# Dilated attention and channel attention on one core: who adds the nine neighbour products

## The chip, the core and the metric

The kernel runs on one core of a Trainium2 chip. Five engines work side by side, each with its own list of instructions, and wait for one another by semaphores: TensorE (PE, matmuls; PEld is its weight load), VectorE (DVE), ScalarE (ACT), GpSimd (POOL) and SyncE (SP, which issues transfers). The metric is the device time of one execution in microseconds (us).

## The reference

`x` is 8 images of 128 channels and 16 by 16 positions. Two residual layers follow each other:

```
x = x + _L0_conv_ref(_gn(x), w_qkv, w_gate, b_gate)
x = x + _L1_conv_ref(_gn(x), W_qkv, b_qkv, W_proj, b_proj)
```

`_gn` is a group norm over groups of 4 channels. The first layer projects to q, k and v (128 channels each), cut into four branches of 32 channels with dilations 1, 2, 4 and 8. In a branch every position looks at a 3 by 3 neighbourhood at that dilation:

```
attn = softmax(einsum('bhdn,bhdkn->bhnk', q, unfold3x3(k)) * scale)
out  = einsum('bhnk,bhdkn->bnhd', attn, unfold3x3(v))
```

The second `einsum` is the place of the change: for each position nine products of a probability and a shifted v are added up. The branch's output is multiplied by a gate (a softmax over the branches of pooled x). The second layer is an attention over channels (heads of 32 channels, 32 by 32 scores), with a projection before and after.

## The kernel before, in words

The 8 images are worked in two halves (`ph` 0 and 1) of four images (`j` 0 to 3). In the first layer a tile's 128 partitions are four images times the 32 channels of one branch `s`, and its free dimension is the 256 positions. One branch of one half is called a **unit** here, written (ph,s).

For a unit, TensorE writes the softmax probabilities, spread over the channels, into PSUM in three chunks (`spread`, L842), one per column shift. VectorE multiplies each chunk with shifted v (`multiply_pv`, L596) and leaves the nine products in the SBUF tile `pv[s]`. Both halves use the same four `pv` tiles. Then eight additions per unit (`additions`, L71) sum the nine products into `acc`: on GpSimd (L333 to L340) or on VectorE (`add_neighbours`, L616). `POOL_SUMS` = (4, 2) says that GpSimd does all four units of half 0 and the first two of half 1; VectorE does (1,2) and (1,3). Outside the middle the shifted windows are smaller where the dilation is larger: the additions cover 240 to 256 elements in branch 0, 224 to 256 in branch 1, 144 or 192 in branch 2 and 64 or 128 in branch 3.

`restore` (L863) brings `acc` back to the layout of the residual, one image per PSUM bank and 128 channels: for each image four matmuls, one per branch, with a 128 by 32 piece of the identity as the weights. Four such matmuls lie side by side in column groups. `first_residual` (L627, two images: one group `g`) adds the image and the result and takes the channel sum. ScalarE takes the sum of squares (`squares`), TensorE averages over the norm's groups (`group_stats`), VectorE computes the variance (`second_variance`, L508 to L516), GpSimd the power -1/2 (`rsqrt`, L302), VectorE the norm's bias (`second_norm_bias`), and ScalarE or VectorE the normed image. From there the second layer runs per group: `project_second`, `transpose`, `attention`, shift, exp and divide, `fuse`, `finish`, `second_residual`, and the store of one image.

Groups 0 and 1 come from half 0 and are worked while half 1 of the first layer still runs; groups 2 and 3 come from half 1, and their chain is the end of the program.

The order on each engine is written out by hand: the lists at L669 to L758 for VectorE and L923 to L1024 for TensorE. On GpSimd it is the loop over halves and units, with `RSQRT_AFTER` naming the addition behind which the `rsqrt` of groups 0 and 1 is put; GpSimd takes its instructions in order, so an addition behind an `rsqrt` waits until that has run. `keep_clock` (L765) are matmuls whose result nobody reads, written where TensorE would otherwise stand idle.

## Time and profile before

| what | value |
|---|---|
| time, median of 3 runs | 84.69 us (84.1 to 85.41) |
| the profiled execution | 84.39 us, its span 82.6 us |
| busy: PE, DVE, ACT, POOL | 67.3, 69.6, 30.7, 42.4 us |
| granted TensorE clock | 1.00 in every slice |
| GpSimd's additions | from 30.84 to 61.88 us |
| first and last addition of VectorE | 59.24 and 65.12 us |
| first matmul of the second `restore` | 65.51 us |

Times in the trace are counted from the start of the span; 1.8 us of the execution's own time lie outside the span. A row gives start and length; rows that follow one another on an engine overlap by some hundredths, since a length holds the pipeline's fill too, so that costs are better taken from start to start. The trace records two matmul rows for each fp32 matmul of the program. "idle before <-releaser" says how long the engine stood and for what.

### The profile page before, as it was taken

To read this page: it belongs to the slowest core of one execution; us is meant where nothing else is said; L and a number is where in the kernel's file an instruction comes from. 1 tells how busy PE (TensorE), PEld (TensorE's weight loads), DVE (VectorE), ACT (ScalarE), POOL (GpSimd) and SP (SyncE) were. 2 spreads that over 40 slices of the span, in tenths; PEclk is the share of its full clock that TensorE was granted. 3 is DMA by queue.
4 is the path that set the end of the run, shared out by engine and by line. 5 is a ranking of instruction groups with operands and counts; after the bars stand their busy time and mean duration, and the time that the engine had idled before them with its cause. 6 is when DMAs were issued, how large, how long until landed. Compare 5 with 4: busy or idle time off the path is not lost.

```text
span 82.6 us, 2228 instructions
## 1 busy us (share of the span) xinstructions
PE 67.3 (81%) x888; PEld 49.0 (59%) x888; DVE 69.6 (84%) x191; ACT 30.7 (37%) x97; POOL 42.4 (51%) x82
## 2 busy tenths in 40 slices
PE   0099899799867979999966797979999787999960
PEld 0099695476433656686855664667685545677830
DVE  1087679999999999999999698889999999857980
ACT  4396599615537000000030004220993155485320
POOL 7104279108700009999999999899990003300000
PEclk9999999999999999999999999999999999999999
DMA  0995004000000000000000000000000000011244
GB/s 5 315 356 150 1 0 100 5 0 0 8 0 0 4 12 0 0 0 0 12 0 0 0 0 0 0 8 0 0 0 0 0 8 4 0 63 64 71 158 159
DMA packets 3019, 3.11 MB, mean 38 GB/s; under 512 B 320, under 2 KB 2752, under 8 KB 3008
## 3 DMA queue, kind: packets, MB, share of 16 engines
q1 hardware_dynamic: 2576, 2.69, 9.9%
q10 hardware_dynamic: 432, 0.26, 1.4%
q8 instruction: 7, 0.11, 0.6%
q14 instruction: 4, 0.03, 0.1%
HBM read 1.91 MB, written 1.05 MB: 36 GB/s over the span
## 4 chain that ended last, share of the span: by engine, by line
DVE 42%; POOL 29%; PE 13%; issue 5%; DMA 4%; ACT 2%; POOLq 1%; ACTq 0%
DVE qk L572 17%; POOL acc L340 13%; POOL pv L340 12%; PE ps L763 11%; DVE pv L613 5%; DMA xt<-x_dram 4%; POOL rstd L305 4%; DVE acc L625 4%; DVE pv L625 3%; DVE x L632 2%; PE ps L898 2%; DVE ssum L589 1%; ACT pT L402 1%; DVE x L658 1%; POOLq L99 1%
## 5 line engine op out<-in xcount | busy, mean ns | idle before, releaser
L763 PE MATMUL ps<-prob,sel 64*128 64x192 f32 (+6 forms) x192 | 17.7, 313 | 2.9 <-DVE pv L613 1.9
L613 DVE TENSOR_TENSOR pv<-ps,v 128x128 f32<-128x128 f32 (+7 forms) x32 | 17.1, 569 | 1.7 <-PE ps L763 0.9
L763 PE MATMUL ps<-xn,wp 128*32 128x256 f32 (+1 forms) x208 | 16.4, 382 | 1.7 <-DVE shifted L582 1.2
L763 PEld LDWEIGHTS ps<-prob,sel 64*128 64x128 f32 x192 | 13.7, 186 | 6.9 <-DVE pv L613 4.8
L340 POOL TENSOR_TENSOR pv<-pv 128x240 f32<-128x240 f32 (+3 forms) x24 | 14.6, 617 | 0.1
L572 DVE TENSOR_TENSOR qk<-q,k 128x720 f32<-128x720 f32 (+7 forms) x24 | 13.9, 646 | 0.1
L763 PE MATMUL ps<-xt 128*128 128x128 f32 x56 | 10.6, 334 | 4.1 <-DMA xt<-x_dram 4.1
L763 PEld LDWEIGHTS ps<-xn,wp 128*32 128x32 f32 (+1 forms) x208 | 9.7, 116 | 6.3 <-DVE shifted L582 1.7
L340 POOL TENSOR_TENSOR acc<-acc,pv 128x256 f32<-128x256 f32 (+4 forms) x20 | 12.6, 635 | 0.5
L305 POOL TENSOR_TENSOR rstd<-gvar,mhalf 128x2 f32<-128x2 f32 (+1 forms) x6 | 4.9, 824 | 14.9 <-DVE gvar L516 14.9
L763 PEld LDWEIGHTS ps<-xt 128*128 128x128 f32 x56 | 8.6, 230 | 5.2 <-DMA xt<-x_dram 4.1
L763 PE MATMUL ps<-qk,cs 128*32 128x192 f32 (+6 forms) x176 | 7.8, 302 | 0.9 <-ACT v L385 0.5
L340 POOL TENSOR_TENSOR acc<-pv 128x256 f32<-128x256 f32 x4 | 2.9, 728 | 8.5 <-DVE pv L613 8.5
L395 ACT ACTIVATE expd<-shifted 128x576 f32<-128x576 f32 x2 | 1.4, 684 | 15.8 <-DVE shifted L582 15.8
L402 ACT ACTIVATE pT<-x 128x256 f32<-128x256 f32 x8 | 3.3, 411 | 10.4 <-DVE x L632 10.4
L763 PEld LDWEIGHTS ps<-qk,cs 128*32 128x32 f32 x176 | 4.7, 109 | 3.6 <-ACT v L385 1.0
L541 DVE TENSOR_REDUCE sums<-xt 128x1 f32<-128x256 f32 x8 | 2.8, 413 | 2.8 <-DMA xt<-x_dram 2.8
L763 PE MATMUL ps<-p,mT 128*128 128x256 f32 x16 | 4.6, 399 | 0.3 <-ACT mT L429 0.2
L763 PE MATMUL ps<-acc,cs 128*32 128x256 f32 x64 | 4.1, 383 | 0.7 <-issue 0.6
L360 ACT ACTIVATE xn<-xt 128x256 f32<-128x256 f32 x8 | 3.2, 404 | 2.0 <-DMA xt<-x_dram 2.0
L415 ACT ACTIVATE p<-ps,wp 128x256 f32<-128x256 f32 x8 | 3.4, 473 | 1.1 <-PE ps L763 1.1
L572 DVE TENSOR_TENSOR qk<-ps,k 128x128 f32<-128x128 f32 (+4 forms) x12 | 3.8, 379 | 0.0
(75 smaller groups left out, 94.0 us busy)
## 6 DMA issues: line engine op xcount, KB each, us to landing
xt<-x_dram SPq DMA_DIRECT2D x4, 256.0 KB, 3.6
out_dram<-x SPq DMA_DIRECT2D x8, 128.0 KB, 1.8
wp<-wpack_dram SPq DMA_DIRECT2D x1, 325.0 KB, 5.6
sel<-selc_dram SPq DMA_DIRECT2D x4, 64.0 KB, 3.9
cs<-consts_dram ACTq DMA_DIRECT2D x1, 130.0 KB, 3.3
cs<-consts_dram ACTq DMA_DIRECT2D x2, 64.0 KB, 2.6
```

Source lines behind the costliest of these rows:

```text
L305: nc.gpsimd.tensor_tensor(rstd[:, bs], gvar[:, bs], mhalf[:, bs], ALU.pow).then_inc(rstd_ready, 1)
L340: nc.gpsimd.tensor_tensor(o, a, b, ALU.add).then_inc(added, 1)
L360: nc.scalar.activation(xn1[:, b // GB, b % GB, :], xt[:, b, :], ACT.Square, accum_out=sums[:, b, 1:2]).then_inc(square_ready, 1)
L402: nc.scalar.activation(pT[:, g, 2 * i:2 * i + 2, :].rearrange("p t n -> p (t n)"), x1[:, b, :], ACT.Square, accum_out=sums1[:, b, 1:2]).th ...
L415: nc.scalar.activation(p1[:, g, i, :], ps[:, BANK[g] + i, 0:N], ACT.Identity, bias=wp[:, W_B1:W_B1 + 1]).then_inc(p1_copied, 1)
L541: nc.vector.tensor_reduce(sums[:, b, 0:1], xt[:, b, :], AX.X, ALU.add).then_inc(sum_ready, 1)
L572: last = nc.vector.tensor_tensor(o, a, b, ALU.mult)
L613: last = nc.vector.tensor_tensor(o, a, b, ALU.mult)
L625: nc.vector.tensor_tensor(o, a, b, ALU.add).then_inc(dve_added, 1)
L632: nc.vector.scalar_tensor_tensor(out=x1[:, b, :], in0=ps[:, BANK[g] + i, 0:N], scalar=1.0, in1=xt[:, b, :], op0=ALU.mult, op1=ALU.add, acc ...
L763: return nc.tensor.matmul(o, w, m, start=start, stop=stop)
L898: last = nc.tensor.transpose(ps[:, BANK[g] + i, P * t:P * t + P], p1[:, g, i, P * t:P * t + P], ident)
```

## The change

Unit (0,3) is no longer added on GpSimd. TensorE adds it: the nine products are matmul operands with the identity as weights, accumulated in PSUM (`sum_units`, `neighbours`). Unit (1,2) goes from VectorE to GpSimd, so that GpSimd does (0,0), (0,1), (0,2), (1,0), (1,1), (1,2), and VectorE only (1,3). `restore` is gone: `sum_units` writes all branches of a half, with 32 by 32 pieces of the identity (32 partitions in, 32 out) instead of 128 by 32. The second `rsqrt` on GpSimd moves in front of unit (1,1). Both residuals of half 0 move forward on VectorE, and 9 of the `keep_clock` matmuls of the later part go: 3 of 6 in front of `spread(1, 0, 0)`, 3 around `spread(1, 2, 2)`, 3 in front of the second sum.

```diff
-POOL_SUMS = (ND, 2)
+POOL_SUMS = (3, 3)
+TENSOR_SUMS = ((3,), ())
-RSQRT_AFTER = ((1, 0, 4), (1, 1, 0))
+RSQRT_AFTER = ((1, 0, 4), (1, 0, 7))
...
+        def neighbours(s):
+            return [(3 * ci + ri, *valid_rows(s, ri), *columns(DIL[s], ci)[:2])
+                    for ci in CENTRE_FIRST for ri in CENTRE_FIRST]
...
-            def restore(g):
...
-                for i in range(GB):
-                    for s in range(ND):
-                        last = mm(ps[32 * s:32 * s + 32, BANK[g] + i, 0:N],
-                                  ident[:, 32 * (first + i):32 * (first + i) + 32], acc[:, ph, s, :])
-                    last.then_inc(restored, 1)
+            def sum_units(ph, units):
+                if ph == 0:
+                    pe.wait_ge(shift_ready, PHASES)
+                    pe.wait_ge(qk_ready, ND * PHASES)
+                else:
+                    pe.wait_ge(pv_ready, 12 * PHASES)
+                parts = []
+                for s in units:
+                    if s in TENSOR_SUMS[ph]:
+                        pe.wait_ge(pv_ready, 12 * ph + 3 * s + 3)
+                        parts.append([(pv[s], slot * N, r0, r1, c0, c1) for slot, r0, r1, c0, c1 in neighbours(s)])
+                        continue
+                    if s < POOL_SUMS[ph]:
+                        pe.wait_ge(added, ADDS * (sum(POOL_SUMS[:ph]) + s + 1))
+                    else:
+                        pe.wait_ge(dve_added, ADDS * (added_before(ph, s) + 1))
+                    parts.append([(acc, (ph * ND + s) * N, 0, H, 0, W)])
+                for n in range(max(len(part) for part in parts)):
+                    for s, part in zip(units, parts):
...
+                        for j in range(SLOTS):
+                            rows = slice(32 * j, 32 * j + 32)
+                            last = mm(view(ps, 512 * (BANK[2 * ph] + j) + r0 * W + c0, dims, 32 * s, 32),
+                                      ident[rows, rows], view(t, offset + r0 * W + c0, dims, 32 * j, 32),
+                                      start=(n == 0), stop=(n == len(part) - 1))
+                            if s == (2, 3)[ph]:
+                                last.then_inc(restored, 1)
...
-            pe.wait_ge(pv_ready, 12 * PHASES)
-            keep_clock(3, BANK[2])
-            restore(2)
-            restore(3)
+            sum_units(1, (0, 1, 2, 3))
```

The instructions move at three places. Each listing gives the line, the operation, output and input, the shape, and the semaphores waited for.

**GpSimd, half 1.** L340 and L350 are the additions, L305 and L315 the `rsqrt` of a group of images. Before, from the first addition of (1,0) on:

```order
L340 TENSOR_TENSOR pv0<-pv0 128x16x15 [waits pv_ready]
L305 TENSOR_TENSOR rstd<-gvar,mhalf 128x2 [waits var_ready]
L340 TENSOR_TENSOR acc<-acc,pv0 128x16x15 [waits added]
L340 TENSOR_TENSOR pv0<-pv0 128x16x15 [waits added]
L340 TENSOR_TENSOR acc<-acc,pv0 128x16x15 [waits added]
L340 TENSOR_TENSOR acc<-pv1 128x256 [waits pv_ready]
L305 TENSOR_TENSOR rstd<-gvar,mhalf 128x2 [waits var_ready]
L340 TENSOR_TENSOR pv1<-pv1 128x16x14 [waits pv_ready]
```

And now:

```order
L350 TENSOR_TENSOR pv0<-pv0 128x16x15 [waits pv_ready]
L315 TENSOR_TENSOR rstd<-gvar,mhalf 128x2 [waits var_ready]
L350 TENSOR_TENSOR acc<-acc,pv0 128x16x15 [waits added]
L350 TENSOR_TENSOR pv0<-pv0 128x16x15 [waits added]
L350 TENSOR_TENSOR acc<-acc,pv0 128x16x15 [waits added]
L315 TENSOR_TENSOR rstd<-gvar,mhalf 128x2 [waits var_ready]
L350 TENSOR_TENSOR acc<-pv1 128x256 [waits pv_ready]
L350 TENSOR_TENSOR pv1<-pv1 128x16x14 [waits pv_ready]
```

The first `rsqrt` keeps its place behind the fifth addition of (1,0), and the second comes one addition earlier; behind unit (1,1) the eight additions on `pv2` follow now.

**VectorE, from the third chunk of (1,0) to the first variance.** L613 and L625 are products, L632 and L644 residuals, L513 to L516 and L523 to L526 the variance. Before:

```order
L613 TENSOR_TENSOR pv0<-ps,v0 128x48x15 [waits spread_ready] x2
L613 TENSOR_TENSOR pv1<-ps,v1 128x768 [waits added,spread_ready,proj_copied]
L632 SCALAR_TENSOR_TENSOR x1,sums1<-ps,xt 128x256 [waits restored] x2
L613 TENSOR_TENSOR pv1<-ps,v1 128x48x14 [waits spread_ready]
L513 TENSOR_TENSOR gst<-ps,signs 128x2x2 [waits gstats_ready]
L515 TENSOR_TENSOR gsq<-gst 128x2 [waits dve_settled]
L516 SCALAR_TENSOR_TENSOR gvar<-gst,gsq 128x2 [waits dve_settled]
```

And now:

```order
L625 TENSOR_TENSOR pv0<-ps,v0 128x48x15 [waits spread_ready] x2
L644 SCALAR_TENSOR_TENSOR x1,sums1<-ps,xt 128x256 [waits restored] x2
L625 TENSOR_TENSOR pv1<-ps,v1 128x768 [waits added,spread_ready,proj_copied]
L644 SCALAR_TENSOR_TENSOR x1,sums1<-ps,xt 128x256 [waits restored] x2
L625 TENSOR_TENSOR pv1<-ps,v1 128x48x14 [waits spread_ready]
L523 TENSOR_TENSOR gst<-ps,signs 128x2x2 [waits gstats_ready]
L525 TENSOR_TENSOR gsq<-gst 128x2 [waits dve_settled]
L526 SCALAR_TENSOR_TENSOR gvar<-gst,gsq 128x2 [waits dve_settled]
```

The residual of group 1 stood behind the first variance and stands in front of it now.

**TensorE, around the third chunk of (1,0).** Before, from `spread(1, 0, 2)` on, which followed `spread(1, 0, 1)` directly:

```order
L763 MATMUL ps<-prob,sel 128x3x4x15 [waits pv_ready]
L763 MATMUL ps<-prob,sel 128x3x4x15 x3
L763 MATMUL ps<-prob,sel 128x3x4x16 [waits pv_ready]
L763 MATMUL ps<-prob,sel 128x3x4x16 x3
L763 MATMUL ps<-acc,cs 32x256 [waits qk_ready,shift_ready,added]
L763 MATMUL ps<-acc,cs 32x256 x7
```

And now:

```order
L774 MATMUL ps<-prob,sel 128x3x4x15 x3
L774 MATMUL ps<-pv3,cs 32x256 [waits pv_ready,qk_ready,shift_ready]
L774 MATMUL ps<-pv3,cs 32x256 x3
L774 MATMUL ps<-pv3,cs 32x128 x8
L774 MATMUL ps<-pv3,cs 32x16x8 x4
L774 MATMUL ps<-pv3,cs 32x8x8 x8
L774 MATMUL ps<-pv3,cs 32x16x8 x4
L774 MATMUL ps<-pv3,cs 32x8x8 x8
L774 MATMUL ps<-prob,sel 128x3x4x15 [waits pv_ready]
L774 MATMUL ps<-prob,sel 128x3x4x15 x3
L774 MATMUL ps<-acc,cs 32x256 [waits added,qk_ready,shift_ready]
L774 MATMUL ps<-acc,cs 32x256 x11
```

The 36 matmuls that add unit (0,3) stand between the second and the third chunk of (1,0), and 12 matmuls for the units (0,0) to (0,2) stand behind the third.

## Rows read from the trace of the kernel before

**Rows 1.** The page: busy time, the span in slices.
```profile
PE 67.3 (81%) x888; PEld 49.0 (59%) x888; DVE 69.6 (84%) x191; ACT 30.7 (37%) x97; POOL 42.4 (51%) x82
...
PEclk9999999999999999999999999999999999999999
```

**Rows 2.** The chain of waits in order of time: start, length, what.
```profile
48.80 0.47 POOL acc L340
...
49.31 0.96 DVE pv L613
...
52.90 0.71 POOL rstd L305
...
63.14 0.79 DVE pv L613 x4
...
65.12 0.29 DVE acc L625
...
66.21 0.86 DVE x L632 x4
...
79.45 0.92 DVE x L658 x2
```

**Rows 3.** Timeline of GpSimd: start, length, engine, line, instruction, tiles.
```profile
36.42 0.73 POOL L340 TENSOR_TENSOR acc<-pv 128x256 f32<-128x256 f32 x1
...
42.27 0.49 POOL L340 TENSOR_TENSOR pv<-pv 128x144 f32<-128x144 f32 x1
...
44.73 0.99 POOL L340 TENSOR_TENSOR pv<-pv 128x144 f32<-128x144 f32 x1
...
45.80 1.00 POOL L340 TENSOR_TENSOR acc<-acc,pv 128x192 f32<-128x192 f32 x2
...
55.68 0.73 POOL L340 TENSOR_TENSOR acc<-pv 128x256 f32<-128x256 f32 x1
...
58.36 1.31 POOL L340 TENSOR_TENSOR pv<-pv 128x224 f32<-128x224 f32 x2
...
59.63 0.80 POOL L340 TENSOR_TENSOR acc<-acc,pv 128x224 f32<-128x224 f32 x1
...
61.20 0.68 POOL L340 TENSOR_TENSOR acc<-acc,pv 128x224 f32<-128x224 f32 x1
```

**Rows 4.** Timeline of VectorE, the second half's products, sums and additions.
```profile
46.46 1.77 DVE L613 TENSOR_TENSOR pv<-ps,v 128x768 f32<-128x768 f32 x2 [0.68 <-issue]
...
48.40 1.87 DVE L613 TENSOR_TENSOR pv<-ps,v 128x720 f32<-128x720 f32 x2 [0.17 <-PE ps L763]
...
50.18 0.41 DVE L632 SCALAR_TENSOR_TENSOR x<-ps,xt 128x256 f32<-128x256 f32 x1
...
51.20 0.86 DVE L613 TENSOR_TENSOR pv<-ps,v 128x672 f32<-128x672 f32 x1 [0.25 <-PE ps L763]
...
52.09 0.16 DVE L513 TENSOR_TENSOR gst<-ps,signs 128x4 f32<-128x4 f32 x1
...
59.82 0.78 DVE L625 TENSOR_TENSOR pv<-pv 128x144 f32<-128x144 f32 x1
...
65.12 0.29 DVE L625 TENSOR_TENSOR acc<-acc,pv 128x128 f32<-128x128 f32 x1
```

**Rows 5.** Timeline of TensorE, matmul rows; x counts two rows a matmul.
```profile
4.05 2.07 PE L763 MATMUL ps<-xt 128*128 128x128 f32 x8 [4.05 <-DMA xt<-x_dram]
...
43.05 1.60 PE L763 MATMUL ps<-xt 128*128 128x128 f32 x12
...
45.43 1.53 PE L763 MATMUL ps<-prob,sel 64*128 64x192 f32 x16 [0.78 <-DVE prob L592]
...
49.31 1.07 PE L763 MATMUL ps<-acc,cs 128*32 128x256 f32 x16
...
63.68 0.33 PE L763 MATMUL ps<-pT 128*32 128x32 f32 x16 [0.20 <-ACT pT L420]
...
65.51 1.93 PE L763 MATMUL ps<-acc,cs 128*32 128x256 f32 x32 [0.58 <-issue]
```

More of the change, by code:

```diff
@@ L244, in of_phase, with added_before @@
             return slice(ph, B, PHASES)
+        def neighbours(s):
+            return [(3 * ci + ri, *valid_rows(s, ri), *columns(DIL[s], ci)[:2])
+                    for ci in CENTRE_FIRST for ri in CENTRE_FIRST]
+        def added_before(ph, s):
+            return len([u for u in range(POOL_SUMS[ph], s) if u not in TENSOR_SUMS[ph]])
         def operands(ph, s, n, target, slot):
@@ L602, in multiply_pv @@
                 dve.wait_ge(spread_ready, c + 1)
-                if ph and chunk == 0:
+                if ph and chunk == 0 and s in TENSOR_SUMS[0]:
+                    dve.wait_ge(restored, SLOTS)
+                elif ph and chunk == 0:
                     dve.wait_ge(added, ADDS * (s + 1))
@@ L608, in multiply_pv @@
                     o = view(pv[s], (3 * ci + ri) * N + r0 * W + c0, [[dri * N + dr * W, n], [W, rows], [1, nc_]])
-                    if ci == 1 and n == 1:
+                    if ci == 1 and n == 1 and s not in TENSOR_SUMS[ph]:
                         o = view(acc, (ph * ND + s) * N, [[W, rows], [1, nc_]])
@@ L616, in add_neighbours @@
             def add_neighbours(ph, s):
-                done = ADDS * (s - POOL_SUMS[ph])
+                done = ADDS * added_before(ph, s)
                 for n, (target, slot, after) in enumerate(additions(s)):
@@ L715, in _ @@
                 multiply_pv(1, 0, i)
+            first_residual(0)
             multiply_pv(1, 1, 0)
-            first_residual(0)
+            first_residual(1)
             multiply_pv(1, 1, 1)
             second_variance(0)
-            first_residual(1)
             multiply_pv(1, 1, 2)
@@ L728, in _ @@
             multiply_pv(1, 3, 0)
-            add_neighbours(1, 2)
             for i in range(1, 3):
@@ L861, in spread @@
                 last.then_inc(spread_ready, 1)
-            def restore(g):
-                ph, first = g // 2, GB * (g % 2)
-                if g % 2 == 0:
-                    pe.wait_ge(added, ADDS * sum(POOL_SUMS[:ph + 1]))
-                    if POOL_SUMS[ph] < ND:
-                        pe.wait_ge(dve_added, ADDS * (ND - POOL_SUMS[ph]))
+            def sum_units(ph, units):
                 if ph == 0:
-                    pe.wait_ge(shift_ready, g + 1)
+                    pe.wait_ge(shift_ready, PHASES)
@@ new lines, in sum_units @@
+                for n in range(max(len(part) for part in parts)):
+                    for s, part in zip(units, parts):
+                        if n >= len(part):
+                            continue
+                        t, offset, r0, r1, c0, c1 = part[n]
+                        dims = [[W, r1 - r0], [1, c1 - c0]]
+                        for j in range(SLOTS):
[5 more added lines that the diff above has]
+                                last.then_inc(restored, 1)
@@ L964, in _ @@
             spread(0, 3, 2)
-            keep_clock(6)
-            for i in range(3):
+            keep_clock(3)
+            for i in range(2):
                 spread(1, 0, i)
-            spread(1, 1, 0)
-            restore(0)
-            spread(1, 1, 1)
+            sum_units(0, (3,))
+            spread(1, 0, 2)
+            sum_units(0, (0, 1, 2))
+            for i in range(2):
+                spread(1, 1, i)
             group_stats(0)
-            restore(1)
             spread(1, 1, 2)
@@ L976, in _ @@
                 spread(1, 2, i)
-            keep_clock(2, BANK[1] + 1)
-            spread(1, 2, 2)
-            keep_clock(1, BANK[1] + 1)
-            spread(1, 3, 0)
             for i in range(2):
                 project_second(0, i)
+            spread(1, 2, 2)
             for i in range(2):
                 project_second(1, i)
-            for i in range(2):
-                transpose(0, i)
-            for i in range(1, 3):
-                spread(1, 3, i)
+            spread(1, 3, 0)
+            transpose(0, 0)
+            spread(1, 3, 1)
+            transpose(0, 1)
+            spread(1, 3, 2)
             transpose(1, 0)
```

1 line of the change is left out of this document (removed).

## The prediction

> **What bounds the kernel now.** I read the page's busy times first: no engine is full, VectorE and TensorE come nearest, and GpSimd works half of the span [rows 1]. So the order of waits counts, and I went on to the chain of waits. From 31.66 on it lies on GpSimd's additions, without a break but for some hundredths, down to the last one of half 0, which ends at 49.27 (48.80 + 0.47). After a detour over the first residuals and their norm it takes GpSimd again from 52.90, and from 57.8 on VectorE with its own additions up to 65.41 (65.12 + 0.29); then follow the residuals of group 2 at 66.21 and the tail, which ends with the last residual, 79.45 + 0.92 [rows 2]. What releases the tail is the first matmul of the second `restore`, at 65.51 [rows 5]: it needs all additions of half 1, on both engines. GpSimd's were done at 61.88 (61.20 + 0.68) [rows 3], so VectorE was late by 3.5 us. The question is when the later of the two is done after the change.
>
> **GpSimd's first saving.** Up to the end of unit (0,2) nothing changes. In the row of two additions at 45.80, which ends at 46.80, the second is the first of unit (0,3) [rows 3]; of the 1.00 I give it 0.41 and the longer one the rest. So (0,2) ends at 46.4, and (0,3) took from there to 49.27: 2.9 us go. Not all of it is won: unit (1,0) needs VectorE's first chunk of it, and the two chunks that begin at 46.46 take 1.77 [rows 4], so the first is there at 47.35. GpSimd starts half 1 at 47.4 in place of 49.22, earlier by 1.8.
>
> **TensorE's new work, and VectorE's delay.** The 36 matmuls of unit (0,3) stand in front of `spread(1, 0, 2)`. No row shows 32 by 32 pieces. Nearest are the 16 matmuls of 256 columns in 1.93 us [rows 5]: less some 0.22 of fill, 0.107 each with four side by side, or 0.43 for a lone one. The windows of unit (0,3) hold 256 + 4 x 128 + 4 x 64 = 1024 columns for each of four images. Side by side that is four times 0.43, 1.7 us; one after the other 6.8. For side by side speaks the row at 45.43, where eight matmuls on the two halves of the partitions, 192 columns each, take 1.53 us: at the lone pace they would need 8 x 0.32 = 2.56 [rows 5]. For the short pieces the issue could bind: 16 rows in 0.33 us [rows 5], so 72 rows want at most 1.5. I take 1.9, lower bound 0 (all of it in gaps of TensorE), upper bound 6.8.
> The Trainium skill, TensorE: Matmul & The Clock Gate, section Measured speedup vs the span model, gives 3.07 times for four row tiles and not 4. An estimate by it from the 6.8 above is 2.2 us, and the sum would be 0.3 higher; no row here shows a row group of 32.
>
> The two spreads of 45.43 have their columns through at 46.75 (1.53 less the fill). Then 1.9 for the sum: 48.65. From the start of `spread(1, 0, 2)` to VectorE's product it was 0.93 (47.47 to 48.40 [rows 4]; 47.47 is the release by the first chunk, at 47.35, and 0.12): 49.6, in place of 48.40. From there VectorE's own list sets the time of the variance of group 0: chunk (1,0,2) 0.91; two residuals 0.77 (two times 0.35 and a readout of 0.08); (1,1,0) 0.96 (the pair of 1.87 less 0.91); two residuals 0.77; (1,1,1) 0.86; the variance 0.74 (52.09 to 52.83) [rows 4]. That is 5.0, so 54.6. Before, it came at 52.83: it had only one pair of residuals in front of it, and no matmuls of unit (0,3). The square sums and `group_stats(0)` come from residuals that are finished at 51.3, three us earlier, and are covered.
>
> **The new wait.** The first `rsqrt` still stands behind GpSimd's fifth addition of (1,0). GpSimd starts sooner, but its fifth addition needs chunk (1,0,2), there at 50.5, and ends at 51.2. Then it stands until 54.65, 3.4 us, where it stood 0.3 before (the `rsqrt` began at 52.90, right after the variance [rows 2]). Queued behind it are three additions of (1,0) and all of (1,1) and (1,2), which need nothing of this norm. The 1.8 us won and more are given back: before, the `rsqrt` began at 52.90, and now at 54.65.
>
> **GpSimd's remaining work.** `rsqrt` 0.71, then three additions: 53.60 to 55.68, 2.1 [rows 2, 3]. Second `rsqrt` 0.71 again; its variance (VectorE at 56) is there before. Units (1,1) and (1,2): the same work in half 0 ran from 36.42 to 46.80, 10.38; less 0.41 of (0,3), and less 0.5 because the addition at 44.73 took 0.99 where its like takes 0.49 at 42.27 [rows 3]: 9.5. Sum 13.0, so 67.6. VectorE's additions of (1,3) fall beside this, since GpSimd is now busy until the end. Beside VectorE's additions GpSimd went from 0.65 (1.27 from 58.36 to 59.63 for two) to 0.79 (59.63 to 61.20 for two) [rows 3]: eight of them cost 0.5 to 1.2; I take 0.5, since these read only 64 or 128 elements. GpSimd ends at 68.1.
>
> **VectorE** loses the eight additions of (1,2), of the kind of the row at 59.82 [rows 4]. That brings nothing at the end, for GpSimd is now the later one. Its last products were through at 63.93 (63.14 + 0.79 [rows 2]) with those eight in front of them; now they have 1.8 us of delay and no such additions, so at 63 at the latest. The eight additions of (1,3) then run against GpSimd: one of 144 elements took 0.78 while GpSimd worked, one of 128 took 0.29 when it was idle [rows 4]. I take it that they keep GpSimd's step and end with it, near 68. The shifts between them and the residuals need 0.8 (65.41 to 66.21 [rows 2]): 68.9.
>
> **The second sum on TensorE** needs 0.5 to 1.0 where 1.93 stood. It is worth nothing: the first image was ready after 0.7 us and VectorE came at 66.21 all the same [rows 2, 5]; the second pair waits for VectorE's `attention_divide`. The last image's ready marker now comes behind all 16 matmuls; 0.1 at most. The tail of 14.2 us (66.21 to 80.37) stays as it is.
>
> **The sum.** Residuals of group 2 at 68.85 in place of 66.21: +2.6. The profiled execution took 84.39, so 87.0. The median of the runs is 84.69, 0.3 above it; I stay at 87.0 and keep the 0.3 in the range. The `keep_clock` matmuls taken out in front of `spread(1, 0, 0)` and `spread(1, 2, 2)` cost nothing, as TensorE waits there for VectorE (0.78 idle at 45.43 [rows 5]); the three at the end are the first rival.
> Bounds of this case: if the sum of (0,3) costs nothing, VectorE is 1.2 earlier, and without the 0.5 of contention the sum is +0.9, 85.3. With 3 us for the sum and 1.2 of contention it is +4.4, 88.8.
>
> **Rivals.**
> *The clock falls.* TensorE's attention of group 1 ended at 64.01 (63.68 + 0.33) [rows 5]; now it ends near 63.7, and nothing stands between it and the sum at 68.1: 4.4 us idle where 0.6 was the most in this part. The granted clock reads 1.00 (2.4 GHz) in all slices [rows 1], so no row shows a fall; but at the start, after 4.05 us of idleness, 8 rows of 128 columns took 2.07 us, and at 43.05 12 rows took 1.60 [rows 5], twice the pace. The tail's matmuls would run at that half pace for a part of 14 us, with 1 to 3 us more on the chain: 88 to 90. The Trainium skill, TensorE: Matmul & The Clock Gate, Part 1, says that an idle stretch takes the clock to half and that activity gives it back; the trace's start agrees, its granted clock does not show it. Chance 0.15.
> *The 32 by 32 pieces run one after another.* Then VectorE's third chunk is another 4.9 later: 91.9. Against it stands the row of 45.43. Chance 0.03.
> *The wait is smaller* (other side: no slower). It decides whether the variance of group 0 is there when the fifth addition ends, at 51.4. If it were, GpSimd would run through: from 47.4, eight additions of (1,0) 5.6, two `rsqrt` 1.4, 9.5 and 0.5 give 64.4, and the residuals could start at 65.2, 1.0 earlier: 83.4. Against it: four blocks of VectorE (residual, product, residual, product) stand between chunk (1,0,2) and the variance. Chance 0.09, of which 0.05 for being under 83.0 by shorter additions.
> *The same mechanism, but small*, since the matmuls of (0,3) overlap with the spreads and additions are not slowed: 85.3 to 86.4. Chance 0.20.
>
> **The numbers.** 2% of 84.69, 1.7 us, is about what a measurement can tell from no change: 83.0 and 86.4. The forecast above 86.4 has 0.53. Slower: 0.53 + 0.15 + 0.03 = 0.71; within 2%: 0.20 + 0.04 = 0.24; faster 0.05. Range 85.2 to 89.2: it leaves out the no-wait case (0.09), the serial case (0.03) and the upper half of the clock case (0.08).
>
> **What would show it.** Right: GpSimd idle some 3 us in front of the first `rsqrt` of group 0, released by the variance on VectorE near 54.6; the matmuls on `pv3` take about 2 us; GpSimd's last addition near 68, and the chain on GpSimd up to it; VectorE's additions of (1,3) at 0.5 or more each. Wrong: if the variance comes before 52.5, if the additions of (1,1) and (1,2) take under 9 us together, or if tail rows (66.21 to 80.37 before) shrink.

## The result and the profile after

The changed kernel takes 90.87 us in the median of its runs (89.19 to 92.54); over the kernel before it stands at 1.0596 (95% interval 1.0415 to 1.0778). The forecast was 87.0 us with a range to 89.2. Medians here are over all runs; the ratios leave disturbed runs out, so a median can stand a little above its ratio. The profiled execution took 90.07 us, its span 88.3, against 84.39 and 82.6 before.

The page of the changed kernel, to be laid beside [rows 1]:

```profile
PE 70.4 (80%) x934; PEld 52.7 (60%) x934; DVE 65.8 (75%) x183; ACT 31.2 (35%) x97; POOL 43.3 (49%) x82
...
PEclk9999999999999999999999999965579975579999
```

TensorE is busy 3.1 us longer, though nine fillers (the `keep_clock` matmuls) are gone and the second sum takes 0.73 us where it took 1.93 (rows below and [rows 5]). The granted clock, 9 in every slice before, falls twice. The windows of the changed kernel say where; the columns are the stretch, its length, busy time and instructions of PE, PEld, DVE, ACT and POOL, the granted clock, the DMA share and GB/s:

```profile
45.60:55.80 10.20, 9.19 (x164) 7.23 (x164) 7.90 (x22) 1.82 (x8) 5.82 (x10) 1.00 0.01 2
55.80:58.50 2.70, 0.00 (x0) 0.00 (x0) 2.70 (x7) 0.61 (x2) 2.62 (x5) 0.92 0.00 0
58.50:65.00 6.50, 6.46 (x25) 4.36 (x26) 0.72 (x2) 2.77 (x6) 6.42 (x11) 0.51 0.00 0
65.00:69.90 4.90, 4.34 (x120) 2.82 (x120) 3.89 (x19) 2.12 (x6) 2.12 (x5) 1.00 0.01 3
69.90:72.00 2.10, 0.56 (x4) 0.56 (x4) 2.03 (x11) 1.05 (x5) 0.00 (x0) 0.94 0.00 0
72.00:78.50 6.50, 6.37 (x21) 5.09 (x20) 4.52 (x20) 2.68 (x10) 1.50 (x2) 0.50 0.12 42
```

No matmul runs from 55.8 to 58.5; behind that the clock is at 1.2 GHz (0.51) for 6.5 us. The same again from 72.00, behind a stretch with 0.56 us of matmuls in 2.1. At the lower clock TensorE is full (6.46 of 6.50, 6.37 of 6.50). VectorE waits for it (0.72 busy of 6.50 in the first stretch); GpSimd doesn't (6.42 of 6.50). The Trainium skill, TensorE: Matmul & The Clock Gate, Part 1, says that idleness takes the clock to half and activity brings it back; both falls agree.

The timeline of the changed kernel on the three engines, in order of time (compare [rows 3, 4, 5]):

```profile
47.02 1.95 PE L774 MATMUL ps<-pv,cs 32*32 32x256 f32 x72
49.84 0.91 DVE L625 TENSOR_TENSOR pv<-ps,v 128x720 f32<-128x720 f32 x1 [1.48 <-PE ps L774]
54.07 0.16 DVE L526 SCALAR_TENSOR_TENSOR gvar<-gst,gsq 128x2 f32<-128x2 f32 x1
54.31 0.71 POOL L315 TENSOR_TENSOR rstd<-gvar,mhalf 128x2 f32<-128x2 f32 x1 [2.78 <-DVE gvar L526]
57.76 0.72 POOL L350 TENSOR_TENSOR acc<-pv 128x256 f32<-128x256 f32 x1
58.54 2.07 PE L774 MATMUL ps<-xn,wp 128*128 128x256 f32 x4 [2.76 <-ACT xn L419]
61.87 0.72 DVE L625 TENSOR_TENSOR pv<-ps,v 128x192 f32<-128x192 f32 x2 [3.38 <-PE ps L774]
65.08 0.42 DVE L625 TENSOR_TENSOR acc<-ps,v 128x256 f32<-128x256 f32 x1 [2.49 <-issue]
66.60 0.59 POOL L350 TENSOR_TENSOR acc<-acc,pv 128x192 f32<-128x192 f32 x1
68.61 0.29 DVE L637 TENSOR_TENSOR acc<-acc,pv 128x128 f32<-128x128 f32 x1
69.05 0.73 PE L774 MATMUL ps<-acc,cs 32*32 32x256 f32 x32 [0.23 <-DVE acc L637]
69.89 0.42 DVE L644 SCALAR_TENSOR_TENSOR x<-ps,xt 128x256 f32<-128x256 f32 x1 [0.21 <-PE ps L774]
71.44 0.56 PE L774 MATMUL ps<-wp,ablk 128*128 128x128 f32 x2 [1.67 <-DVE ablk L661]
85.15 0.92 DVE L670 SCALAR_TENSOR_TENSOR x<-ps,wp,x 128x256 f32<-128x256 f32 x2 [0.20 <-PE ps L774]
```

Up to 57.76 this is the forecast: the sum of (0,3), the late third chunk, the late variance, GpSimd standing 2.78 us. Then it leaves it. `project_second` waits for ScalarE's normed image, late because the `rsqrt` was late, and the list has put `spread(1, 2, 2)` and `spread(1, 3, 0)` behind it. This move is part of the change too, though its description above leaves it out: before, both spreads stood ahead of `project_second`. VectorE waits 3.38 us, and again 2.49, for products forecast to be through at 63. They are at 67.43 (66.94 + 0.49), later than GpSimd's last addition (67.19, 66.60 + 0.59). So what sets the end of half 1 is VectorE, which TensorE kept waiting for its products, and not GpSimd. Residuals of group 2 start at 69.89, 3.68 after 66.21 [rows 2]; from there to the end of the last one it is 16.18 us (86.07) where it was 14.16 [rows 2]: 2.0 more. The sum is 5.7, the growth of the span.

### The profile page after: what moved, and what is told of

It reads as the page before. It is cut to its first block, busy times and chain, and to the rows that moved or that the text cites. A ratio compares the mean times of both kernels' runs of the same rounds, so it can differ in the third digit from the quotient of the medians.

```text
span 88.3 us, 2314 instructions
## 1 busy us (share of the span) xinstructions
PE 70.4 (80%) x934; PEld 52.7 (60%) x934; DVE 65.8 (75%) x183; ACT 31.2 (35%) x97; POOL 43.3 (49%) x82
## 4 chain that ended last, share of the span: by engine, by line
DVE 46%; PE 41%; issue 5%; DMA 3%; ACT 2%; ACTq 0%
PE ps L774 39%; DVE qk L582 19%; DVE pv L625 12%; DMA xt<-x_dram 3%; DVE ssum L599 2%; PE ps L923 2%; DVE x L644 2%; DVE smax L589 2%; DVE srec L600 1%; DVE prob L602 1%; DVE x L670 1%; DVE acc L637 1%; DVE gsq L525 1%; DVE acc L625 1%; ACT xn L419 1%
## 5 line engine op out<-in xcount | busy, mean ns | idle before, releaser
L774 PE MATMUL ps<-xn,wp 128*32 128x256 f32 (+1 forms) x208 | 19.9, 413 | 4.0 <-ACT xn L419 2.8
L625 DVE TENSOR_TENSOR pv<-ps,v 128x128 f32<-128x128 f32 (+7 forms) x33 | 17.4, 563 | 6.4 <-PE ps L774 5.5
L774 PE MATMUL ps<-prob,sel 64*128 64x192 f32 (+6 forms) x192 | 19.0, 327 | 3.1 <-DVE pv L625 1.5
L774 PEld LDWEIGHTS ps<-xn,wp 128*32 128x32 f32 (+1 forms) x208 | 12.9, 129 | 8.0 <-ACT xn L419 2.9
L350 POOL TENSOR_TENSOR pv<-pv 128x240 f32<-128x240 f32 (+2 forms) x24 | 15.2, 643 | 0.5 <-DVE pv L625 0.3
L350 POOL TENSOR_TENSOR acc<-acc,pv 128x192 f32<-128x192 f32 (+3 forms) x20 | 13.0, 656 | 0.5
L315 POOL TENSOR_TENSOR rstd<-gvar,mhalf 128x2 f32<-128x2 f32 (+1 forms) x6 | 4.9, 824 | 15.4 <-DVE gvar L526 15.4
L774 PE MATMUL ps<-xt 128*128 128x128 f32 x38 | 8.1, 366 | 3.8 <-DMA xt<-x_dram 3.8
L774 PEld LDWEIGHTS ps<-xt 128*128 128x128 f32 x38 | 6.6, 257 | 4.6 <-DMA xt<-x_dram 3.8
L350 POOL TENSOR_TENSOR acc<-pv 128x256 f32<-128x256 f32 x4 | 2.9, 728 | 9.6 <-DVE pv L625 9.6
L774 PE MATMUL ps<-wp,ablk 128*128 128x128 f32 x16 | 3.6, 364 | 1.7 <-DVE ablk L661 1.7
L774 PEld LDWEIGHTS ps<-wp,ablk 128*128 128x128 f32 x16 | 2.8, 242 | 2.4 <-DVE ablk L661 2.3
L430 ACT COPY pT<-ps 128x256 f32<-128x256 f32 x8 | 2.8, 371 | 3.5 <-PE ps L923 3.5
```

Source lines behind the costliest of these rows:

```text
L315: nc.gpsimd.tensor_tensor(rstd[:, bs], gvar[:, bs], mhalf[:, bs], ALU.pow).then_inc(rstd_ready, 1)
L350: nc.gpsimd.tensor_tensor(o, a, b, ALU.add).then_inc(added, 1)
L430: nc.scalar.copy(pT[:, g, 2 * i:2 * i + 2, :].rearrange("p a n -> p (a n)"), ps[:, BANK[g] + i, 0:N]).then_inc(pT_copied, 1)
L625: last = nc.vector.tensor_tensor(o, a, b, ALU.mult)
L774: return nc.tensor.matmul(o, w, m, start=start, stop=stop)
```

## Experiments

Two theories stood at the start. **Clock**: the forecast mechanism stands, some 2.4 us, and the rest is TensorE at the lower clock, in the middle and in the tail, since the work that kept it busy has gone. **Order**: the two spreads behind `project_second` are the cost, whatever the clock.

**1. Fill the gap in the middle.** `keep_mid` is the changed kernel and

```diff
+            keep_clock(9, BANK[1] + 1)
             for i in range(2):
                 project_second(0, i)
```

> The changed kernel with nine matmuls that nobody reads in front of project_second(0, 0), where TensorE stood from 55.8 to 58.5. Clock theory: the granted clock stays at 1.00 from 58 to 66, the three waits of VectorE's products for the spreads (1,2,2), (1,3,0) and (1,3,2), 6.3 us in sum now, shrink to 3 to 4, and the second sum starts near 67.7 in place of 69.05; time 1 to 1.5 us under the changed kernel's. Order theory (the loss there is that spread(1, 2, 2) and spread(1, 3, 0) stand behind matmuls that wait for ScalarE's norm): VectorE still waits 5 us or more, and the time stays within 0.5 us.

Measured: 90.24 us, 1.0644 (1.0543 to 1.0745): nothing won. Its windows:

```profile
55.80:66.90 11.10, 9.18 (x130) 6.78 (x129) 7.50 (x22) 5.13 (x12) 10.86 (x19) 1.00 0.01 1
66.90:76.80 9.90, 7.24 (x52) 5.49 (x53) 8.04 (x36) 3.27 (x14) 1.80 (x3) 0.54 0.01 2
```

And the second sum in its timeline:

```profile
67.76 1.17 PE L774 MATMUL ps<-acc,cs 32*32 32x256 f32 x32 [2.02 <-DVE acc L637]
```

The first fall is gone, TensorE is through earlier, and now it stands 2.02 us in front of the second sum, where it stood 0.23: the second fall begins some 5 us sooner, and the stretch at 0.54 is 9.9 us long, where 6.5 us at 0.50 stood. By itself, filling the first gap only moves the loss.

**2. Fill the gaps in the tail too.** `keep_both` is `keep_mid` and

```diff
+            pe.wait_ge(pv_ready, 12 * PHASES)
+            keep_clock(3, BANK[2])
             sum_units(1, (0, 1, 2, 3))
+            pe.wait_ge(ashift_ready, 1)
+            for _ in range(5):
+                mm(ps[:, BANK[0], 384:512], xt[:, 0, 0:P], xt[:, 0, 0:P])
             fuse(0, 0)
```

> As keep_mid, and besides three such matmuls in front of the second sum (as the kernel before has them) and five behind it. Clock theory: the granted clock is 1.00 to the end, the stretch from the first residual of group 2 to the last residual, 16.2 us in the changed kernel, goes back to 14.2, and the time is 3 to 3.5 us under the changed kernel's, near 87. If the tail is longer for another reason than the clock, it stays at 16.

Measured: 86.77 us, 1.0264 (1.0166 to 1.0361). Windows and timeline of `keep_both`:

```profile
68.60:83.00 14.40, 12.60 (x126) 9.16 (x126) 11.75 (x48) 6.95 (x27) 1.50 (x2) 1.00 0.16 54
```

```profile
68.65 0.42 DVE L644 SCALAR_TENSOR_TENSOR x<-ps,xt 128x256 f32<-128x256 f32 x1 [0.21 <-PE ps L774]
81.79 0.92 DVE L670 SCALAR_TENSOR_TENSOR x<-ps,wp,x 128x256 f32<-128x256 f32 x2 [0.20 <-PE ps L774]
```

The clock is 1.00 in the stretch, and 0.999 over the execution; this is the kernel that I had forecast: residuals at 68.65 (forecast 68.85), tail 14.06 (82.71 less 68.65), 86.8 us (forecast 87.0). A part of the agreement is luck: GpSimd was done at 67.25, 0.9 sooner than forecast, and VectorE, held up by products that the forecast had on time, at 67.66. By the ratios (1.0596 less 1.0264) the falls cost 3.3%, 2.8 us; between the spans of the two profiled executions it is 3.4. `keep_tail` has the lines of this diff alone:

> The changed kernel with the fillers around the second sum alone. If the two falls of the clock are separate costs: the first (58 to 65) stays, with the second sum near 69 to 70, the tail goes back to 14.2 us, and the time is near 88.5, 2 us under the changed kernel. If a fall only moves (as with keep_mid, where filling the first gap let the second fall come sooner): over 89.5.

Measured: 89.11 us, 1.0437 (1.0369 to 1.0505), 1.6% less than the changed kernel. Its windows show the fall in the middle left and the one in the tail away:

```profile
58.00:66.00 8.00, 6.36 (x26) 4.27 (x26) 2.43 (x8) 3.38 (x7) 7.92 (x14) 0.57 0.00 0
71.00:79.00 8.00, 7.13 (x78) 5.27 (x66) 6.48 (x30) 4.45 (x18) 1.50 (x2) 1.00 0.03 9
```

The tail, from the first residual of group 2 to the last one, takes 14.07 us again (71.27 to 85.34), so this part of the cost can be taken away by itself. In the profiled execution a third fall, from 46 to 50 (0.71), comes ahead of these two; experiment 6 returns to it.

**3. The order alone.** `order_nokeep` is the changed kernel with `spread(1, 2, 2)` and `spread(1, 3, 0)` in their old place, and no filler:

```diff
                 spread(1, 2, i)
+            spread(1, 2, 2)
+            spread(1, 3, 0)
             for i in range(2):
                 project_second(0, i)
-            spread(1, 2, 2)
...
-            spread(1, 3, 0)
```

> The changed kernel with spread(1, 2, 2) and spread(1, 3, 0) back in front of the projections, and no matmul added. Both theories: VectorE's waits of 3.4 and 2.5 us go, since TensorE does these spreads in the gap. Order theory: the second sum starts at 67.5, set by GpSimd, and the clock falls only in the tail; time 1.5 us under the changed kernel's. Clock theory: TensorE still has gaps before the norm is there, the clock may fall near 60, and then the gain is under 1 us.

Measured: 87.90 us, 1.0375 (1.03 to 1.045). By the ratios 2.2 of the 6.0% go, 1.9 us: more than the clock theory allowed for it (under 1), and nearer to the order theory's 1.5. VectorE has its chunk without a wait, and waits for the next. The timeline of VectorE, and a window:

```profile
58.64 0.71 DVE L625 TENSOR_TENSOR pv<-ps,v 128x192 f32<-128x192 f32 x2
...
63.40 0.93 DVE L625 TENSOR_TENSOR pv<-ps,v 128x128 f32<-128x128 f32 x4 [3.40 <-PE ps L774]
```

```profile
58.00:60.00 2.00, 2.00 (x14) 1.62 (x11) 2.00 (x7) 1.90 (x4) 2.00 (x5) 0.56 0.00 0
```

The clock falls all the same, here and in the tail (0.50 from 70 to 74). Order and clock are two causes on the same stretch: mending either takes part of the same wait away, and the sizes are not to be added. What the order costs at full clock, the table in experiment 8 shows: 0.25 us.

**4. The nine fillers in the kernel before.** `before_nokeep` is the kernel before, and

```diff
-            keep_clock(6)
+            keep_clock(3)
...
-            keep_clock(2, BANK[1] + 1)
             spread(1, 2, 2)
-            keep_clock(1, BANK[1] + 1)
...
-            keep_clock(3, BANK[2])
             restore(2)
```

> The kernel before, without the nine matmuls that the change takes out. Clock theory: these alone hold the clock in the later part; it falls in one place at least and the kernel is 1 to 3 us slower. Otherwise (the fall needs the change's long waits): the same time within 0.5 us and the clock at 1.00.

Measured: 86.34 us, 1.0187 (1.0099 to 1.0275). Windows, and the two gaps in the timeline of TensorE:

```profile
46.90:51.00 4.10, 4.10 (x30) 3.72 (x32) 2.30 (x5) 0.00 (x0) 3.94 (x11) 0.58 0.00 0
...
66.00:68.00 2.00, 0.35 (x20) 0.27 (x24) 1.93 (x12) 0.00 (x0) 0.00 (x0) 0.92 0.00 0
68.00:70.00 2.00, 2.00 (x21) 0.99 (x24) 0.93 (x6) 0.77 (x3) 0.00 (x0) 0.50 0.03 8
```

```profile
46.86 4.61 PE L763 MATMUL ps<-prob,sel 64*128 64x192 f32 x32 [1.46 <-DVE prob L592]
...
67.88 2.74 PE L763 MATMUL ps<-acc,cs 128*32 128x256 f32 x21 [1.65 <-DVE acc L625]
```

The fillers matter at two places; around `spread(1, 2, 2)` the clock stays at 1.00 without its three (53 to 66). With three fewer in front of `spread(1, 0, 0)` TensorE stands 1.46 us there, where it stood 0.78, and the spreads of (1,0) take 4.61 us where they took 1.53 and 1.73. Without the three in front of the second `restore` it stands 1.65 where it stood 0.58 [rows 5]. Behind each gap the clock is down. What I had costed at nothing is worth 1.6 us in the kernel before, together with the tail's three; no run parts the two.

**5. The smaller pieces alone.** `before_pieces` is the kernel before, its `restore` in 32 by 32 pieces:

```diff
-                    for s in range(ND):
-                        last = mm(ps[32 * s:32 * s + 32, BANK[g] + i, 0:N],
-                                  ident[:, 32 * (first + i):32 * (first + i) + 32], acc[:, ph, s, :])
+                for s in range(ND):
+                    for i in range(GB):
+                        rows = slice(32 * (first + i), 32 * (first + i) + 32)
+                        last = mm(ps[32 * s:32 * s + 32, BANK[g] + i, 0:N], ident[rows, rows], acc[rows, ph, s, :])
```

> The kernel before, with nothing changed but the pieces of the identity in the restoring matmuls: 32 by 32, branch by branch, in place of 128 by 32. Side by side theory: the 16 matmuls of the second restore take 0.8 us in place of 1.93, VectorE comes at 66.2 all the same, the time is within 0.5 us of the kernel before, unless TensorE's shorter work lets the granted clock fall, which would show as 0.50 near 70 and 0.5 to 2 us.

Measured: 87.67 us, 1.0368 (1.0314 to 1.0422), a surprise: it makes TensorE's own work shorter. Timeline and windows:

```profile
49.32 0.67 PE L763 MATMUL ps<-acc,cs 32*32 32x256 f32 x16
51.67 0.36 PE L763 MATMUL ps<-sums,cs 128*128 128x4 f32 x2 [0.92 <-ACT pT L402]
66.59 0.71 PE L763 MATMUL ps<-acc,cs 32*32 32x256 f32 x32
```

```profile
49.00:52.00 3.00, 1.95 (x37) 1.11 (x36) 2.70 (x7) 0.91 (x4) 3.00 (x6) 1.00 0.00 0
52.00:59.00 7.00, 6.85 (x52) 5.18 (x52) 5.24 (x17) 1.32 (x5) 6.54 (x10) 0.51 0.01 2
69.30:75.50 6.20, 6.07 (x21) 5.08 (x20) 4.74 (x22) 2.16 (x9) 1.50 (x2) 0.50 0.06 22
```

The first sum of two images takes 0.67 where it took 1.07 [rows 5], the second of four 0.71 for 1.93. TensorE has 1.95 us of work in the 3.0 from 49 on, with no gap above 0.92, and the clock falls behind it. The second fall, from 69.3, stands behind a gap of 1.59 us (67.3 to 68.9) in the place of the shorter second sum. `pieces_keep` gives the work back as fillers (the five in front of `fuse(0, 0)` as in experiment 2):

```diff
             restore(0)
+            keep_clock(2, BANK[1] + 1)
             spread(1, 1, 1)
+            keep_clock(2, BANK[1] + 1)
...
             group_stats(1)
+            keep_clock(2, BANK[1] + 1)
```

> before_pieces with eleven more matmuls that nobody reads: two behind the first restore, two behind spread(1, 1, 1), two behind group_stats(1), five behind the last restore. Clock theory (the pieces cost time only by leaving TensorE less work, so that the granted clock falls from 52.5 to 59 and from 69.5 to 76): the clock stays at 1.00 and the time goes back from 87.7 to within 0.5 us of the kernel before. Rival (32 by 32 pieces cost time by themselves, by switching the array or by the four markers): it stays 1 us or more above.

Measured: 84.81 us, 0.9997 (0.9949 to 1.0046), the clock at 1.00. The pieces cost nothing and bring nothing; the 3.7% were the clock.

**6. The wait of the first `rsqrt`.** `keep_rsqrt` is `keep_both` with

```diff
-RSQRT_AFTER = ((1, 0, 4), (1, 0, 7))
+RSQRT_AFTER = ((1, 1, 0), (1, 1, 2))
```

> The kernel of keep_both (clock held), with GpSimd's two rsqrt moved behind the first and the third addition of unit (1,1). GpSimd theory (with the clock held, what is left of the loss, 1.9 us, is GpSimd standing 2.8 us before the rsqrt of group 0): that wait falls under 0.5, GpSimd ends near 64.5, the second sum starts near 65.5 to 66 and the time is 1.5 to 2 us under keep_both, the same as the kernel before within 1%. Order theory (VectorE's waits for the spreads of (1,2) and (1,3) are as late as GpSimd): VectorE's last product is at 64.3 there whatever GpSimd does, its eight additions need 1.5 us more, and the gain ends at 1.5 us.

Measured: 87.34 us, 1.031 (1.0254 to 1.0366), no gain; but its clock fell at another place. A window of `keep_rsqrt`:

```profile
46.00:50.00 4.00, 4.00 (x88) 3.24 (x86) 1.86 (x2) 0.00 (x0) 1.81 (x4) 0.71 0.00 0
```

TensorE's list is the changed kernel's up to here, and so is the gap ahead of it: 1.43 us in front of the spreads at 45.21, where the changed kernel's profiled execution has 1.44 at 45.56 and keeps its clock. So the three fillers taken out in front of `spread(1, 0, 0)` leave a place where the clock falls in some executions and not in others. Of the six of `keep_rsqrt` five stood at 0.98 of the clock; the one at 1.00 took 86.26 us, 0.5 under `keep_both`. That is one execution and settles little. `spreads_first` is `keep_rsqrt` with

```diff
-            keep_clock(9, BANK[1] + 1)
-            for i in range(2):
-                project_second(0, i)
             spread(1, 2, 2)
...
             spread(1, 3, 0)
+            keep_clock(5, BANK[1] + 1)
+            project_second(0, 0)
             spread(1, 3, 1)
+            project_second(0, 1)
             spread(1, 3, 2)
+            for i in range(2):
+                project_second(1, i)
```

and `spreads_first_3_2` has unit (1,2) on VectorE besides (`POOL_SUMS = (3, 2)`, and `add_neighbours(1, 2)` ahead of `add_neighbours(1, 3)`).

> keep_rsqrt, with all spreads of (1,2) and (1,3) in front of the matmuls that wait for ScalarE's norms. Order theory: VectorE's products are through at 61 in place of 64.3, GpSimd's end near 64.7 sets the second sum, and the time is 0.5 to 1 us under keep_rsqrt. GpSimd theory: GpSimd's end decides in keep_rsqrt already, and nothing changes.

> spreads_first, with unit (1,2) added on VectorE as in the kernel before; unit (0,3) stays on TensorE. If the additions of (1,2) were well placed on VectorE: GpSimd ends near 60.5, VectorE's sixteen additions run from 61 to 64.5 without it, and the second sum starts at 64.5, as in spreads_first or 0.3 earlier. If moving (1,2) to GpSimd was right: 1 us later than spreads_first.

They came to 88.45 us, 1.0403 (1.0331 to 1.0474), and 87.81 us, 1.0338 (1.0278 to 1.0399), both at 0.96 of the clock in the profiled execution, low between 56 and 63 (0.54 and 0.52). They settle nothing.

So `held` gives TensorE work everywhere. It is `spreads_first` with

```diff
-            keep_clock(3)
+            keep_clock(6)
...
             group_stats(1)
+            keep_clock(2, BANK[1] + 1)
             for i in range(2):
                 spread(1, 2, i)
+                keep_clock(2, BANK[1] + 1)
             spread(1, 2, 2)
             spread(1, 3, 0)
-            keep_clock(5, BANK[1] + 1)
+            keep_clock(4, BANK[1] + 1)
```

and `held_stall` is `held` with `RSQRT_AFTER` as in the change.

> The change with all that the runs so far found wrong in it mended at once: the six matmuls in front of spread(1, 0, 0) as before, fillers behind group_stats(1) and between the spreads, all spreads of (1,2) and (1,3) in front of what waits for ScalarE, both rsqrt in unit (1,1), fillers around the second sum. GpSimd runs from 47.5 without a long wait and ends near 65; VectorE's last addition near 64.8; the second sum at 65.2; clock 1.00. Time 84.0 to 84.6, the same as the kernel before within 0.5 us. If it is over 86 with the clock at 1.00, something in the change is still not understood.

> held with one difference: the two rsqrt where the change has them. GpSimd theory: GpSimd stands 2.8 us before the first, ends near 67.2, the time is 1.5 to 2.3 us over held. Order theory: under 0.5 us over held, since VectorE's products decide.

Measured: `held` 85.58 us, 1.0111 (1.007 to 1.0151); `held_stall` 87.0, 1.0267 (1.0207 to 1.0326). Timeline of GpSimd, first `held_stall`, then `held`:

```profile
54.12 0.71 POOL L315 TENSOR_TENSOR rstd<-gvar,mhalf 128x2 f32<-128x2 f32 x1 [2.78 <-DVE gvar L526]
...
66.67 0.58 POOL L350 TENSOR_TENSOR acc<-acc,pv 128x192 f32<-128x192 f32 x1
```

```profile
54.52 0.71 POOL L315 TENSOR_TENSOR rstd<-gvar,mhalf 128x2 f32<-128x2 f32 x1 [0.29 <-DVE gvar L526]
...
64.33 0.60 POOL L350 TENSOR_TENSOR acc<-acc,pv 128x192 f32<-128x192 f32 x1
```

The wait is 2.78 with the `rsqrt` early and 0.29 with it late, GpSimd is done 2.32 us sooner, and the kernel is 1.6% faster, 1.3 us. The clock doesn't explain it: it was 0.975 in the profiled execution of `held_stall` and 0.995 in that of `held`, but three executions of `held_stall` stood at 1.00 of the clock and took 86.51, 86.85 and 87.32 us, and of the eight of `held` at 1.00 seven took 85.27 to 85.90 and one 88.14.

**7. A filler can itself be late.** `held_late` is `held` and

```diff
             pe.wait_ge(pv_ready, 12 * PHASES)
-            keep_clock(3, BANK[2])
             sum_units(1, (0, 1, 2, 3))
```

> held without the three fillers in front of the second sum, which stood behind attention(1) and so put the sum off from 65.66 to 66.53 while the last additions were done at 65.5. If the filler was on the path: the sum starts at 65.7, the residuals of group 2 at 66.5 in place of 67.4, and the time is 0.7 to 0.9 us under held, the same as the kernel before. If the clock falls without them: as held or slower, with the granted clock at 0.50 near 68.

Measured: 84.78 us, 1.0043 (1.0022 to 1.0064), 0.7% less than `held`. In `held` the fillers ran from 65.66, VectorE's last addition was done at 65.54, and the sum began only at 66.53:

```profile
65.25 0.29 DVE L637 TENSOR_TENSOR acc<-acc,pv 128x128 f32<-128x128 f32 x1
...
65.66 0.94 PE L774 MATMUL ps<-xt 128*128 128x128 f32 x6
66.53 0.71 PE L774 MATMUL ps<-acc,cs 32*32 32x256 f32 x32
```

**8. What do the moved units bring?** `held_no03` is `held_late` with unit (0,3) on GpSimd:

```diff
-POOL_SUMS = (3, 3)
-TENSOR_SUMS = ((3,), ())
+POOL_SUMS = (4, 3)
+TENSOR_SUMS = ((), ())
...
-            sum_units(0, (3,))
             spread(1, 0, 2)
-            sum_units(0, (0, 1, 2))
...
+            spread(1, 1, 0)
+            sum_units(0, (0, 1, 2, 3))
```

and the residual of group 0 in its old place on VectorE; that of group 1 stands behind chunk (1,1,1), still ahead of the variance. The four units of half 0 are summed at once, behind `spread(1, 1, 0)`. `held_3_2` and `held_late_3_2` are `held` and `held_late` with (1,2) on VectorE, in the way of `spreads_first_3_2`.

> held_late without the sum of unit (0,3) on TensorE: GpSimd adds (0,3) as in the kernel before and (1,2) too. If taking (0,3) from GpSimd is worth what it leaves free there: GpSimd starts half 1 at 49.2 in place of 47.5 and ends 1.7 us later, near 66.7, the time is 1.2 to 1.8 us over held_late. If it is worth nothing (VectorE's wait for its third chunk takes it back): within 0.5 us of held_late.

> held with unit (1,2) added on VectorE. GpSimd ends near 60.5, VectorE's sixteen additions run from 60.8 to 64.4 by themselves, and the second sum starts near 64.8: 0 to 0.5 us under held. If VectorE's additions meet GpSimd's they take 0.7 each and it is 0.5 us over.

> held_late with unit (1,2) added on VectorE. Where the second half's adding is done would not matter: the sixteen additions of VectorE end near 65 without GpSimd beside them, within 0.4 us of held_late. It is 0.5 us over or more if VectorE's own list is the longer one.

Measured: `held_no03` 86.33 us, 1.0127 (1.0089 to 1.0165), 0.8% over `held_late`. `held_late_3_2` 85.5 us, 1.0133 (1.0082 to 1.0184), 0.9% over `held_late`. `held_3_2`, 85.76 us and 1.0098 (1.0058 to 1.0138), stands no higher than `held`. Timeline and window of `held_no03`, then the timeline of `held_late`:

```profile
26.77 0.82 DVE L602 SCALAR_TENSOR_TENSOR prob<-expd,gate,srec 128x576 f32<-128x576 f32 x1
65.89 1.17 PE L774 MATMUL ps<-acc,cs 32*32 32x256 f32 x32 [1.02 <-DVE acc L637]
```

```profile
66.00:68.00 2.00, 2.00 (x36) 1.19 (x35) 1.40 (x8) 0.69 (x4) 0.00 (x0) 0.51 0.00 0
```

```profile
27.43 0.82 DVE L602 SCALAR_TENSOR_TENSOR prob<-expd,gate,srec 128x576 f32<-128x576 f32 x1
66.36 0.73 PE L774 MATMUL ps<-acc,cs 32*32 32x256 f32 x32
```

The two executions are 0.66 us apart at 27, where their programs are still the same. Counted from the probabilities of half 0 (these rows at 27, L592 in the kernel before), the profiled executions divide into a way to the second sum and the rest:

| kernel | probabilities | second sum | between | sum to end of span |
|---|---|---|---|---|
| before | 26.81 | 65.51 | 38.70 | 17.1 |
| changed | 26.95 | 69.05 | 42.10 | 19.3 |
| `keep_both` | 26.80 | 67.81 | 41.01 | 17.1 |
| `held_stall` | 26.75 | 67.51 | 40.76 | 17.9 |
| `held` | 26.87 | 66.53 | 39.66 | 17.2 |
| `held_3_2` | 27.91 | 67.59 | 39.68 | 17.1 |
| `held_late` | 27.43 | 66.36 | 38.93 | 17.1 |
| `held_late_3_2` | 26.64 | 66.13 | 39.49 | 17.2 |
| `held_no03` | 26.77 | 65.89 | 39.12 | 17.9 |

With unit (0,3) on TensorE the second sum comes 0.2 us sooner (38.93 against 39.12); the other 0.8 us of `held_no03` stand behind the sum, at 0.51 of the clock. So the move itself is worth little: GpSimd is done 0.75 us sooner by it, VectorE only 0.3. Unit (1,2) on GpSimd is worth 0.6 us (38.93 against 39.49, both at full clock); `held` and `held_3_2` don't show it, since their three late fillers cover it. These are single executions. No version was faster than the kernel before.

## Why the prediction was wrong

The direction, the mechanism up to 57.76 and the clock as a danger were right; the size was 3.9 us short, since the clock's term was put at nothing.

- **The sum of (0,3) on TensorE**: 1.9 forecast, 1.95 measured for 36 matmuls. The pieces run side by side; the serial rival is out. Against 6.8 us, the prediction's estimate for one after the other, that is 3.5 times faster. The estimate of 2.2 from the Trainium skill, TensorE: Matmul & The Clock Gate, section Measured speedup vs the span model, was 0.25 too long.
- **VectorE's delay**: third chunk 49.6 forecast, 49.84 measured; variance done at 54.6, measured 54.23 (54.07 + 0.16).
- **The new wait**: 3.4 forecast, 2.78 measured. GpSimd's fifth addition ended at 51.53 and not at 51.2, and the `rsqrt` began at 54.31 and not at 54.65. `held_stall` against `held` shows that the wait reaches the end, with 1.3 us; against `held_late`, whose sum no filler puts off, it is 1.8 (40.76 less 38.93).
- **GpSimd's end**: 68.1 forecast, 67.19 measured. Units (1,1) and (1,2) took 9.43 (57.76 to 67.19) where I had 9.5 and another 0.5 of contention. The contention did not come, since VectorE's additions stood behind GpSimd's (67.35 to 68.90). It came in `keep_both`, where they ran together: 0.60 for 128 elements at 65.00, and 0.29 at 67.37, when GpSimd was done.
- **The failed step**: "The `keep_clock` matmuls taken out in front of `spread(1, 0, 0)` and `spread(1, 2, 2)` cost nothing, as TensorE waits there for VectorE". They stood there because TensorE waits there: an idle TensorE was what I had to price, and I priced it at 0. In the kernel before, taking three away in front of `spread(1, 0, 0)` is enough for a fall (`before_nokeep`: 0.58 behind 1.46 us of idleness). With the change the same gap is as wide (1.44 at 45.56); the clock stays at 1.00 behind it in the profiled execution, and falls to 0.71 in that of `keep_rsqrt`. Around `spread(1, 2, 2)` the late norm opens 2.76 us, in front of 58.54, and the clock falls to 0.51. With nine fillers there and eight around the second sum the time is 86.77, the forecast. So the mechanism was right, and the clock's term was 0 where 2.8 us stood, the tail's share included. Whether the three fillers of that place would have been enough for the wider gap, no run shows.
- **The second sum**, "needs 0.5 to 1.0 where 1.93 stood. It is worth nothing": true for the path (0.73 us for 16 matmuls against 1.93), wrong for the clock. Shorter sums are less work: in the changed kernel TensorE stands 1.67 us behind the second one, where it stood 0.40, and in `before_pieces` the smaller pieces alone drop the clock and cost 3.7%.
- **The rival "The clock falls"** had the cause and too little of it. I looked for one gap, 4.4 us in front of the second sum. It was 0.23, since the products came late; once the middle is filled it is there (2.02 in `keep_mid`). The falls of the changed kernel begin with 2.76 us in the middle and 1.67 behind the sum. The 1 to 3 us fit the tail alone (2.0 to 2.1). Chance 0.15 was too little: [rows 1] show the clock at 1.00, and I read that as safe instead of asking what holds it.
- **What I left out**: `spread(1, 2, 2)` and `spread(1, 3, 0)` now stand behind `project_second`, which waits for the norm that I had made late myself. "At 63 at the latest" for VectorE's products took in no wait for TensorE; they were through at 67.43. In `keep_both`, in the same order at full clock, VectorE still waits, but its last addition is done at 67.66, near GpSimd's forecast end. At full clock the order costs 0.25 us (`keep_both` 41.01 in the table, `held_stall` with the spreads in front 40.76); it costs much only together with the low clock.
- **Where the time went**: of the 5.7 us between the spans of before and after, 2.4 are what the forecast named (residuals at 68.65 in `keep_both` against 66.21), 1.2 come from the low clock ahead of the residuals (69.89 against 68.65), and 2.1 from it behind them (16.18 against 14.06; before, this was 0.1 more). Of the 1.2, 0.15 stand already at 27, ahead of any change.
- **What is left at full clock**: `keep_both` reaches the second sum 2.3 us later than the kernel before (41.01 against 38.70). By the table 0.25 of them are the order, 1.8 GpSimd's wait for the early `rsqrt`, and 0.2 are left in `held_late`. Each step compares single executions, and the fillers differ between the kernels, so the shares are good to some tenths.

Not shown: which of the missing fillers cost how much, and why the clock falls behind the gap at 45 in some executions only.

## What to carry to other kernels

A clock that reads 1.00 everywhere is a state that something holds: before taking fillers out, or making TensorE's work shorter, ask of every gap on TensorE around the edit what fills it, and look at the granted clock behind it. When a norm or a statistic becomes late, follow each engine's list to what stands behind its consumer, on every engine. Fillers are matmuls in the queue like others: nine missing ones cost 1.9%, three that were late 0.7%. And before a difference of under 1% is put down to a move, align the traces at a row that the edit can't have touched, and see on which side of the edit the time lies.
